# Routing one batch row ahead of the other in a mixture-of-experts stage, with part of its search moved into the attention before it

## The chip, the cores and the metric

One core of one Trainium2 chip runs the whole program in one launch. The metric is the device time of the execution in microseconds (us), the median of three runs. Engines: PE (TensorE), VectorE (DVE in the rows), ScalarE (ACT), GpSimd (POOL) and SyncE (SP); 16 DMA engines move data.

## What is computed

Two batch rows of 1,024 tokens with 128 features pass four residual layers: attention a, a mixture-of-experts feed-forward, attention b, the same feed-forward again. Both attentions have 16 heads of 8 features and are causal.

```python
x = x + attn_a(layernorm(x));  x = x + ffn(layernorm(x))
x = x + attn_b(layernorm(x));  x = x + ffn(layernorm(x))

def ffn(x):                                     # 8 experts, hidden 512
    scores = softmax(einsum('bsd,ed->bse', x, router_w))
    gate, sel = top_k(swapaxes(scores, 1, 2), 257)      # 257 tokens per expert and row
    tokens = x[b, sel]
    h = gelu(tokens @ w1 + b1)
    y = (h @ w2 + b2) * gate[..., None]
    return zeros_like(x).at[b, sel].add(y)
```

An expert takes 257 of the 1,024 tokens of each row. The choice is a top-k over tokens, so nothing can be gathered before all scores of a row are known.

## The kernel before

The kernel writes out the order of each engine by hand. It runs per layer k (0 for a, 1 for b) `project_and_attend` and then `feed_forward`, each a block with its own PSUM banks.

**Attention.** A layer has 16 halves (`HALVES`): a group of four heads of one batch row by the upper or lower 512 queries. A half is 12 or 28 units, 320 in a layer; the second row starts at unit 160, and offsets below are counted from there. A unit is one score product (L1055), one exp on ScalarE (L1141), and every four units the values product (L1073) for a set of keys. Ahead of the scores PE computes all scores once more to find row maxima: pieces (L993), reduced on VectorE (L1164), over a ring of two slots of two PSUM banks (`RINGS`, `mx`). `beside_table` places the pieces; the last of them stands at offset 122. Output turns and the projection of the first row use the ring too. In layer a `PROJECT` puts the first row's projection at offsets 132 and 138, with join, measurement and normalise (L1207, L418 to L451) behind; in layer b the first row's joins, measurements, scale and normalise stand at offset 148.

**Feed-forward: the front.** The normalised input is turned by PE (`turn`, L1443), copied and split in two parts for the fp32r products, and multiplied with the router weights (`logits`, L1450). `keep_busy` (L499) puts idle matmuls in the gaps. Then softmax.

**Search and lists.** Both rows are searched together: 15 steps (`SHIFTS`), each eight small PE products that count (L1466), two VectorE instructions that take the count (L1784, L1786) and two that set up the next one (L1774, L1776). `rank` settles ties, `place` numbers the slots, `make_hot` (L1824, 2,048 elements) lays out one expert's one-hot lanes and `find` (L1507) reads its row numbers. GpSimd gathers by them: first the 257th tokens of all experts (`odd_x`, L1413), then each expert's four index columns (L1400).

**Items.** Three experts are computed densely on all 2,048 tokens, twelve items of 512 (`("dense", q)`, turned back and weighted by a gate that is zero for tokens not chosen, L1847). Five are routed: `("some", s)` holds 258 slots of both rows, in two halves. The order is ten dense, five routed, two dense. An item is four hidden blocks (L1587 dense, L1594 routed) and, after the next item's hidden blocks, four output blocks (L1610, L1615). A block is three products, high by high, high by low, low by high; the units of the stage count blocks, eight per item. ScalarE applies gelu (L1659) and makes the high part (L1666), VectorE the low part (`low`, L1735), which the output waits for. `rows_low`, `scale_back` serve the routed items.

**Two spare banks** carry everything else that PE computes beside the items (`SPARE_AT`): a wait on `spare_done` ahead of each entry. `SPARE_AT` and `vector_events` fix at which unit each entry stands, on PE, ScalarE and VectorE alike; all three work strictly in that order.

**Weights** are in three buffers each; experts 3 to 7 wait until a predecessor has been used.

**The end.** GpSimd adds scaled rows to a DRAM sum (L1408, four per expert, each waiting for the expert before it), then the odd rows (L1422). SP and ScalarE reload the sum (L1391), VectorE adds it to x (L1895), and in layer b SP stores the output.

## Time and profile before

| | us |
|---|---|
| median of 3 runs (978.05 to 980.05) | 979.27 |
| the profiled execution | 978.48 |
| its span | 976.6 |
| PE busy | 840.6 (86%) |
| VectorE busy | 653.0 (67%) |
| ScalarE busy | 565.9 (58%) |
| GpSimd busy | 350.9 (36%) |

A program reads each engine's busy time from one profiled execution. Matmuls overlap in the records, so the mean of one is longer than the distance from one to the next: the distance is what a stretch of products costs, and it is read from the chain, where pieces follow each other without overlap. An idle engine costs nothing by itself; it costs where every other engine waits as well. The stages, by the first and last instruction of each: feed-forward of layer a 336.4 to 506.7, of layer b 810.3 to 976.6.

### The profile page before, as it was taken

To read this page: it belongs to the slowest core of one execution; us is meant where nothing else is said; L and a number is where in the kernel's file an instruction comes from. 1 tells how busy PE (TensorE), PEld (TensorE's weight loads), DVE (VectorE), ACT (ScalarE), POOL (GpSimd) and SP (SyncE) were. 2 spreads that over 40 slices of the span, in tenths; PEclk is the share of its full clock that TensorE was granted. 3 is DMA by queue.
4 is the path that set the end of the run, shared out by engine and by line. 5 is a ranking of instruction groups with operands and counts; after the bars stand their busy time and mean duration, and the time that the engine had idled before them with its cause. 6 is when DMAs were issued, how large, how long until landed. Compare 5 with 4: busy or idle time off the path is not lost. (4 is left out here: it accounts for less than half of the span.)

```text
span 976.6 us, 15787 instructions
## 1 busy us (share of the span) xinstructions
PE 840.6 (86%) x5786; PEld 535.1 (55%) x5786; DVE 653.0 (67%) x1204; ACT 565.9 (58%) x1020; POOL 350.9 (36%) x579
## 2 busy tenths in 40 slices
PE   3888999999999889979937898999999988997992
PEld 1554566556655567769824333444444436676981
DVE  4686667767774457947745877777777745785772
ACT  2524666656666567746705256666666676775661
POOL 1262336656233300186826112133212330008683
PEclk9999999999999989989969799999999999997996
DMA  3662431331111151024424271110000006112444
GB/s 102 185 204 55 143 85 66 98 98 34 66 66 45 59 160 44 22 70 132 54 53 125 69 186 43 34 34 13 22 2 2 1 2 185 55 44 57 138 56 100
DMA packets 57595, 73.57 MB, mean 75 GB/s; under 512 B 11296, under 2 KB 44784, under 8 KB 57136
## 3 DMA queue, kind: packets, MB, share of 16 engines
q1 hardware_dynamic: 43024, 61.42, 21.5%
q0 software_dynamic: 7168, 5.45, 4.2%
q10 hardware_dynamic: 7328, 5.71, 2.1%
q8 instruction: 46, 0.75, 0.3%
q14 instruction: 29, 0.24, 0.1%
HBM read 41.68 MB, written 29.77 MB: 73 GB/s over the span
## 5 line engine op out<-in xcount | busy, mean ns | idle before, releaser
L1141 ACT ACTIVATE b_pt<-b_banks 128x512 f32<-128x512 f32 (+1 forms) x320 | 154.6, 559 | 100.1 <-PE b_banks L1055 99.9
L1164 DVE TENSOR_REDUCE a_mlate<-a_banks 128x2 f32<-128x1024 f32 (+3 forms) x120 | 125.0, 1080 | 50.8 <-PE a_banks L993 32.1
L1164 DVE TENSOR_REDUCE b_mlate<-b_banks 128x2 f32<-128x1024 f32 (+3 forms) x120 | 126.0, 1081 | 35.0 <-PE b_banks L993 18.3
L1055 PE MATMUL a_banks<-a_q,a_k 121*128 121x512 f32 (+3 forms) x384 | 117.4, 383 | 5.5 <-DMA a_q<-a_mt 4.6
L1141 ACT ACTIVATE a_q_hl<-a_banks 128x512 f32<-128x512 f32 (+1 forms) x160 | 81.8, 557 | 68.5 <-PE a_banks L1055 67.0
L1141 ACT ACTIVATE a_k_hl<-a_banks 128x512 f32<-128x512 f32 (+1 forms) x160 | 82.2, 557 | 52.8 <-PE a_banks L1055 51.3
L993 PE MATMUL a_banks<-a_k,a_q 120*128 120x512 f32 (+3 forms) x384 | 99.5, 362 | 11.0 <-DVE a_mlate L1164 7.3
L1055 PE MATMUL b_banks<-b_q,b_k 64*128 64x512 f32 (+3 forms) x384 | 98.1, 413 | 11.7 <-ACT b_pt L1141 8.9
L1659 ACT ACTIVATE f_h<-f_banks,b_t 128x512 f32<-128x512 f32 (+1 forms) x136 | 89.4, 685 | 30.3 <-PE f_banks L1594 17.0
L1055 PEld LDWEIGHTS b_banks<-b_q,b_k 64*128 64x128 f32 x384 | 47.1, 185 | 86.7 <-ACT b_pt L1141 55.3
L1055 PEld LDWEIGHTS a_banks<-a_q,a_k 121*128 121x128 f32 x384 | 65.3, 191 | 50.9 <-issue 20.1
L1610 PE MATMUL f_banks<-f_hr,f_w2r 128*128 128x512 f32 x288 | 81.5, 416 | 6.4 <-DVE f_hr L1735 6.4
L1735 DVE TENSOR_TENSOR f_hr<-f_h,f_hr 128x1024 fp32r<-128x1024 f32 (+1 forms) x68 | 82.8, 1220 | 3.6 <-ACT f_hr L1666 3.5
L919 POOL TENSOR_SCALAR_AFFINE_SELECT b_pt<-b_pt 128x128 f32<-128x128 f32 x128 | 36.9, 293 | 133.9 <-ACT b_pt L1141 133.8
L993 PE MATMUL b_banks<-b_k,b_q 63*128 63x512 f32 (+3 forms) x384 | 75.1, 381 | 9.8 <-DVE b_mlate L1164 6.1
L1587 PE MATMUL f_banks<-f_xr,f_w1r 128*128 128x512 f32 x288 | 80.3, 418 | 0.6 <-ACT f_h L1659 0.6
L1073 PE MATMUL b_banks<-b_pt,vg 128*32 128x512 f32 (+3 forms) x768 | 79.9, 506 | 0.0
L993 PEld LDWEIGHTS a_banks<-a_k,a_q 120*128 120x128 f32 x384 | 64.6, 192 | 26.0 <-DVE a_mlate L1164 15.7
L1408 POOL DMA_INDIRECT scratch_sum<-f_xg,f_index x40 | 69.4, 1735 | 20.6 <-issue 10.4
L1666 ACT ACTIVATE f_hr<-f_h 128x1024 fp32r<-128x1024 f32 (+1 forms) x68 | 72.2, 1062 | 2.2
L1164 DVE TENSOR_REDUCE b_mearly<-b_banks 128x2 f32<-128x768 f32 (+3 forms) x56 | 49.7, 918 | 24.5 <-PE b_banks L1003 23.8
L1164 DVE TENSOR_REDUCE a_mearly<-a_banks 128x2 f32<-128x768 f32 (+3 forms) x56 | 49.7, 916 | 21.9 <-PE a_banks L1003 21.1
(252 smaller groups left out, 1371.0 us busy)
## 6 DMA issues: line engine op xcount, KB each, us to landing
scratch_w<-a_tab SPq DMA_DIRECT2D x16, 512.0 KB, 3.0
f_w1r<-scratch_w SPq DMA_DIRECT2D x16, 512.0 KB, 4.5
f_w2r<-scratch_w SPq DMA_DIRECT2D x16, 512.0 KB, 3.6
a_rot<-in_w SPq DMA_DIRECT2D x16, 256.0 KB, 3.9
a_q<-scratch_q SPq DMA_DIRECT2D x8, 384.0 KB
a_k<-scratch_k SPq DMA_DIRECT2D x8, 384.0 KB
scratch_q<-b_q_hl SPq DMA_DIRECT2D x24, 128.0 KB, 2.8
b_q<-scratch_q SPq DMA_DIRECT2D x32, 96.0 KB
```

Of the source, the lines that this page charges most:

```text
L919: pool.affine_select(out=block[:, 0:P], in_=block[:, 0:P], compare_op=ALU.is_ge, fill=0.0, base=0, pattern=[[1, P]], channel_multiplier=-1 ...
L993: last = pe.matmul(to[:, bank, col:col + w], head_rows(q2, n, h, slice(q * P, (q + 1) * P), 0), head_rows(k2, n, h, slice(k0, k0 + w), 0), ...
L1055: last = pe.matmul(st[u % NST][:, col:col + w], head_rows(k2, n, h, slice(key * P, (key + 1) * P), 1), head_rows(q2, n, h, slice(c * CH + ...
L1073: last = pe.matmul(o_ps[VW * h:VW * (h + 1), q0:CH], vg[n % 2][:, key, h, :], pt[(SET0[i] + s) % NPT][:, h, col:col + w], start=(key == 0) ...
L1141: act.activation(pt[at % NPT][:, h, 0:cols], st[u % NST][:, 0:cols], ACT.Exp, scale=scale).then_inc(exp_done, 1)
L1164: last = dve.tensor_reduce(dst, src, AX.X, ALU.max, negate=True)
L1408: pool.indirect_dma_start(out=sums, out_offset=row(s, c), in_=xg[s][:, c, 0:D], in_offset=None, compute_op=ALU.add).then_inc(scattered[c / ...
L1587: last = pe.matmul(h_ps[:, j, :], w[:, wp, j * P:(j + 1) * P], xr[xp][:, chunk(c)], start=(p == 0), stop=(p == 2))
L1610: last = pe.matmul(y_ps[:, n % 2, :], w[:, wp, j * P:(j + 1) * P], hr[n % 2][hp][:, j, 0:CH], start=(j == 0 and p == 0), stop=(j == HB - 1 ...
L1659: act.activation(to, source, ACT.Gelu, bias=m.b1_t[:, e * HB + j:e * HB + j + 1]).then_inc(gelu_done, 1)
L1666: act.activation(hr[n % 2][0][:, j - 1:j + 1, 0:width], h[n % 2][:, j - 1:j + 1, 0:width], ACT.Copy).then_inc(h_high, 1)
L1735: dve.tensor_tensor(hr[q % 2][1][:, first:end, 0:width], h[q % 2][:, first:end, 0:width], hr[q % 2][0][:, first:end, 0:width].bitcast(F32) ...
```

## The change

Batch row 0 is routed apart from row 1, and ahead of it.

- In the attention's last third (`ROUTE_AT`, `ROUTE_VECTOR`, `ROUTE_SCALAR`, offsets of the second row) the first row goes through projection (layer a, offsets 108 and 111), joins and measurements (110 to 114), scale (115), normalise on ScalarE (117 to 120), turning (123), logits (127), exp (129), softmax and first step (130), and 11 of 15 search steps (133 to 158). The entries use the ring. Its rows and scores are stored to DRAM there, and the sums zeroed.
- Both rows have two dense experts and six routed ones: 8 dense items and 12 routed of 258 columns instead of 12 and 5 of twice 258. Steps are done per row, on half the columns, so 30 in place of 15 in a layer.
- Order: four dense of row 0, six routed of row 0, three dense of row 1, six routed of row 1, one dense.
- The front is gone. The second row's attention output, norm, turning and logits are entries beside the first items (units -1 to 20), its 15 steps start at unit 22, its list is laid out at unit 76 (the first row's at unit 18).
- Lists are made from two digits of 16 (`lists`, `find`, `expand`) for all experts of a row at once; `make_hot` is gone.
- All eight experts' weights have buffers of their own and load in one go. There are two DRAM sums per row, so a scatter waits for the expert before the last, and two DMAs per expert in place of four. The first row's sum is reloaded and added before the last output.
- `keep_busy` is gone from the feed-forward.

The core of the diff:

```diff
-KEEP = 3
-DENSE = KEEP * NCH
-ROUTED = NE - KEEP
...
-AHEAD = 10
-
-ITEMS = [("dense", q) for q in range(AHEAD)] + [("some", s) for s in range(ROUTED)]
-ITEMS += [("dense", q) for q in range(AHEAD, DENSE)]
+DIGITS = 16
+QUAD = 4
+LATE = range(NCH // B, NCH)
+KEEPS = (2, 2)
+
+ITEMS = [("dense", 0, 0), ("dense", 0, 1), ("dense", 1, 0), ("dense", 1, 1)] + [("some", 0, e) for e in range(KEEPS[0], NE)]
+ITEMS += [("dense", 0, 2), ("dense", 0, 3), ("dense", 1, 2)] + [("some", 1, e) for e in range(KEEPS[1], NE)] + [("dense", 1, 3)]
 ITEM = {item: n for n, item in enumerate(ITEMS)}
+SOME = [item for item in ITEMS if item[0] == "some"]
+SOME_AT = {item: i for i, item in enumerate(SOME)}
+KEPT = [item for item in ITEMS if item[0] == "dense"]
+KEPT_ROOM = 4
+TAKE_AT = {(4, 1): 2, (4, 3): 3}
...
+SOME_COST, DENSE_COST, STEP_COST, STEP_EVERY = 0.65, 0.95, 0.4, 2.1
+EARLY_STEPS = 11
+STEPS = len(SHIFTS)
+
...
+def spare_table(k):
+
+    at = [(-1, ("attn", 2)), (-1, ("attn", 3)), (0, ("through", 2)), (1, ("through", 3))] if k == 0 else []
+    for n, item in enumerate(ITEMS):
+        if item[0] == "some":
+            late = 0 if ITEMS[n - 1][0] == "some" else 2
+            at += [(unit_of(n - 1) + 3 + late, ("rows", *item[1:])), (unit_of(n + 2) + 1, ("back", *item[1:]))]
+    first = [(2 * i - 1, ("count", 0, EARLY_STEPS + i)) for i in range(STEPS - EARLY_STEPS)]
+    u = first[-1][0]
+    at += first + [(u + 2, ("rank", 0)), (u + 4, ("place", 0)), (u + 5, ("odd_index", 0)), (u + 11, ("find", 0)),
+                   (u + 13, ("expand", 0))]
+    at += [(13, ("xn", 2)), (14, ("xn", 3)), (18, ("logits", 1))]
+    steps = paced(22, [STEP_EVERY] * (STEPS + 1) + [1.0, 4.5, 1.2])
+    at += [(u, ("count", 1, i)) for i, u in enumerate(steps[:STEPS])]
+    at += list(zip(steps[STEPS:], [("rank", 1), ("place", 1), ("odd_index", 1), ("find", 1), ("expand", 1)]))
+    last = {b: max(ITEM["some", b, e] for e in range(KEEPS[b], NE)) for b in range(B)}
+    after = unit_of(last[0] + 2)
+    at += [(unit_of(6) + 3, ("twins", 0)), (after + 5, ("odd_turn", 0)), (after + 7, ("odd_sum", 0))]
+    for i, item in enumerate(KEPT):
+        b = item[2] // (NCH // B)
+        n = 5 + i if b == 0 else last[0] + 3 + i
+        at.append((max(unit_of(n) + 5, unit_of(ITEM[item] + 2) + 3), ("turn", i)))
+    after = unit_of(last[1] + 2)
+    at += [(unit_of(last[1] - 3) + 5, ("twins", 1)), (after + 3, ("odd_turn", 1)), (after + 4, ("odd_sum", 1))]
+    return sorted(at, key=lambda entry: entry[0])
...
+def vector_events(k):
 
     events = []
     for n in range(len(ITEMS)):
-        for at, first in zip(low_units(n), (0, 2)):
-            events.append((at, 1, "low", (n, first, first + 2)))
-    for i in range(len(SHIFTS)):
-        events.append((FIRST_COUNT + i * COUNT_EVERY, 0, "step", i))
-    events.append((RANK, 0, "rank", 0))
-    events.append((PLACE, 0, "place", 0))
-    for u, keys in BESIDE_UNIT.items():
-        events += [(u, 2 + i / 10, key[0], key[1:]) for i, key in enumerate(keys)]
-    events += [(u, 3, "hot", s) for s, u in HOT_AT.items()]
-    events += [(100, 3, "odd_spread", ()), (112, 3, "odd_gates", ())]
+        for at, first in zip((4, 6), (0, 2)):
+            events.append((unit_of(n) + at, 1, "low", (n, first, first + 2)))
+    events += [(-1, 4, "split", (0,)), (1, 4, "split", (1,)), (unit_of(4) + 5, 4, "split", (2,)), (unit_of(4) + 7, 4, "split", (3,))]
+    if k:
+        events.append((0, 1.5, "join", (2,)))
+    events += [(3, 4, "measure", (2,))] + [(5, 4, "measure", (3,))] * (k == 0)
+    events += [(7, 4, "scale", ()), (8, 4, "norm", (2,)), (8, 5, "norm", (3,))]
+    at = {key: u for u, key in SPARE_AT[k]}
+    for b in range(B):
+        events += [(at["place", b], 3, "lists", (b,)), (at["twins", b] - 5, 4, "odd_spread", (b,)),
...
+ROUTE_AT = {"a": [(108, ("attn_turn", 0)), (111, ("attn_out", 0))], "b": []}
+for _kind in "ab":
+    ROUTE_AT[_kind] += [(123, ("xn_turn", 0)), (127, ("logits", 0))]
+    ROUTE_AT[_kind] += [(133 + 5 * i // 2, ("count", i)) for i in range(EARLY_STEPS)]
+ROUTE_VECTOR = {"a": [(113, "measure", 0), (114, "measure", 1), (115, "scale", 0), (130, "weigh", 0)],
+                "b": [(110, "join", 0), (111, "measure", 0), (112, "join", 1), (113, "measure", 1), (115, "scale", 0),
+                      (130, "weigh", 0)]}
+ROUTE_SCALAR = [(117 + i, "norm", i) for i in range(TT // 2)] + [(129, "exp", 0)]
...
+    def lists(self, dve):
+
+        m = self.m
+        dve.tensor_scalar(m.high_digit[:, :, :], m.slot[:, :, :], 4, None, ALU.logical_shift_right)
+        self.link(dve, dve.tensor_scalar(m.low_digit[:, :, :], m.slot[:, :, :], DIGITS - 1, None, ALU.bitwise_and))
+        numbers = m.steps[:, len(SHIFTS) * PLANES:].rearrange("p (o n) -> p o n", o=1).to_broadcast([P, TT * NE, DIGITS])
+        digit = lambda t: t.rearrange("p t (e o) -> p (t e) o", o=1).to_broadcast([P, TT * NE, DIGITS])
+        self.link(dve, dve.tensor_tensor(self.pairs[:, :, 1, :], numbers, digit(m.high_digit[:, :, :]), ALU.is_equal))
+        dve.tensor_tensor(self.ends, numbers, digit(m.low_digit[:, :, :]), ALU.is_equal)
+        self.link(dve, dve.tensor_scalar(self.pairs[:, :, 0, :], self.pairs[:, :, 1, :], m.token[:, 0:1], None, ALU.mult))
+        ones = self.pairs.rearrange("p (t e) v a -> p t e v a", e=NE)[:, :, :, 1, :]
+        rows = m.tile_row[:, :].rearrange("p (t o q) -> p t o q", o=1, q=1)
+        dve.tensor_tensor(ones, ones, rows.to_broadcast([P, TT, NE, DIGITS]), ALU.mult).then_inc(m.hot_ready, 1)
...
+        early.store_rows(sp, norm)
+        early.store_scores(sp)
+        for b in range(B):
+            for to in m.sums["ab".index(kind)][b]:
+                sp.dma_start(to[0:T, :].rearrange("(t p) d -> p t d", p=P),
...
+        def norm_tiles(first, end):
+
+            act.wait_ge(norm.scaled, NCH // B)
+            for t in range(first, end):
+                act.activation(m.xn[:, t, :], m.x[:, t, :], ACT.Identity, scale=m.sc[:, 2, t:t + 1], bias=m.sc[:, 3, t:t + 1]
+                               ).then_inc(norm.xn_by_act, 1)
...
+        early.wait_lists(pool)
+        early.gather_odd(pool)
+        for e in experts[0]:
+            gather(0, e)
+        pool.wait_ge(m.filled, 16 * 4 * (k + 1))
+        for e in experts[0][:-2]:
+            scatter(0, e)
+        late.wait_lists(pool)
+        late.gather_odd(pool)
+        gather(1, experts[1][0])
+        gather(1, experts[1][1])
+        scatter(0, NE - 2)
+        gather(1, experts[1][2])
+        scatter(0, NE - 1)
+        for e in experts[1][3:]:
+            gather(1, e)
+        scatter_odd(0)
+        for e in experts[1]:
+            scatter(1, e)
+        scatter_odd(1)
...
+        beside(-1)
+        for u in range(LAST_UNIT):
+            n, j = divmod(u + HB, 2 * HB) if u >= HB else (0, u)
+            if j < HB and n < len(ITEMS):
+                hidden(n, j)
+            elif j >= HB:
+                output(n - 1, j - HB)
+            beside(u)
+        for u in range(LAST_UNIT, LAST_UNIT + 2 * HB):
+            beside(u)
...
+        def finish(b):
+            for c in range(b * NCH // B, (b + 1) * NCH // B):
+                dve.wait_ge(m.x_in[c], 32 * (k + 1))
+                early.link(dve, dve.tensor_tensor(flat(m.x, c), flat(m.x, c), landing(c, 0).rearrange("p t n -> p (t n)"), ALU.add))
+                dve.tensor_tensor(flat(m.x, c), flat(m.x, c), landing(c, 1).rearrange("p t n -> p (t n)"), ALU.add
+                                  ).then_inc(finished, 1)
```

`Routing` holds a row's chain (projection to lists) for both places it is called from; each of its counts, `rank` and `place` is an entry of the ring in the attention and of the spare banks in the feed-forward.

## Rows read from the trace of the kernel before

**Rows 1.** The page, busy time: engine, us (share of the span) x instructions.
```profile
PE 840.6 (86%) x5786; PEld 535.1 (55%) x5786; DVE 653.0 (67%) x1204; ACT 565.9 (58%) x1020; POOL 350.9 (36%) x579
```

**Rows 2.** Busy time by stretch: from:to, length, each engine, granted clock, DMA.
```profile
745.00:780.00 35.00, 31.89 (x242) 14.49 (x240) 25.39 (x33) 21.92 (x47) 8.67 (x27) 1.00 0.01 2
336.40:506.70 170.30, 142.09 (x975) 115.94 (x975) 108.90 (x247) 101.58 (x140) 65.11 (x42) 0.91 0.34 85
810.30:824.00 13.70, 13.18 (x104) 11.45 (x104) 9.69 (x38) 8.04 (x16) 0.00 (x0) 1.00 0.79 232
824.00:887.10 63.10, 58.96 (x410) 44.14 (x410) 49.75 (x102) 50.51 (x68) 8.40 (x3) 0.97 0.23 70
887.10:892.40 5.30, 0.00 (x0) 0.00 (x0) 0.25 (x1) 0.52 (x1) 4.08 (x5) 0.63 0.16 40
892.40:957.80 65.40, 64.40 (x447) 56.13 (x447) 43.23 (x89) 41.44 (x56) 50.34 (x34) 0.95 0.40 84
957.80:976.60 18.80, 0.63 (x4) 0.42 (x4) 3.71 (x8) 0.00 (x0) 3.77 (x3) 0.56 0.49 121
```

**Rows 3.** The chain of waits at the first gather, layer b: start, us, what.
```profile
877.31 0.78 issue
878.09 4.49 POOL f_odd_x L1413
882.88 3.17 POOL f_xg L1400
886.35 1.83 POOL f_xg L1400
889.75 2.59 DMA f_xg<-scratch_x,f_index
```

**Rows 4.** The chain at the end of the program.
```profile
966.28 5.44 DMA v<-scratch_sum
```

**Rows 5.** The chain: a search step, three dense products, twelve routed, four transposes.
```profile
855.26 0.22 DVE f_planes L1784
...
856.62 1.14 DVE f_hr L1735
...
861.87 0.70 PE f_banks L1587 x3
...
910.00 0.44 PE f_banks L1554 x4
...
915.25 1.45 PE f_banks L1594 x12
```

**Rows 6.** Busy time by stretch: joins, measurements, scale of layer b's first row.
```profile
786.30:793.60 7.30, 6.00 (x39) 1.93 (x31) 6.63 (x33) 5.04 (x11) 1.23 (x5) 1.00 0.00 0
```

**Rows 7.** The exps (L1141) alone, by stretch of attention b: ACT busy (x count).
```profile
745.00:780.00 35.00, 21.19 (x45) 1.00 0.01 2
780.00:805.00 25.00, 17.41 (x37) 0.96 0.01 2
```

**Rows 8.** Groups by line and shape: count | busy us, mean ns | idle before.
```profile
L1164 DVE TENSOR_REDUCE b_mlate<-b_banks 128x2 f32<-128x1024 f32 x80 | 96.9, 1223 | 21.9 <-PE b_banks L993 18.3 <-PE b_banks L1003 3.7
L1824 DVE TENSOR_TENSOR f_hot<-steps,f_lane 128x2048 bf16<-128x2048 int32 x10 | 22.8, 2280 | 0.1
L1847 DVE SCALAR_TENSOR_TENSOR x<-f_banks,f_gate,x 128x128 f32<-128x128 f32 x96 | 27.0, 344 | 16.4 <-PE f_banks L1554 16.0
L1141 ACT ACTIVATE b_pt<-b_banks 128x256 f32<-128x256 f32 x64 | 20.7, 389 | 18.9 <-PE b_banks L1055 18.8
L444 ACT ACTIVATE xn<-x,sc 128x128 f32<-128x128 f32 x32 | 13.1, 482 | 7.4 <-DVE sc L436 7.4
```

**Rows 9.** DMA issues: what, queue, count, size, median us from issue to landing.
```profile
f_w1r<-scratch_w SPq DMA_DIRECT2D x16, 512.0 KB, 4.5
```

**Rows 10.** Timeline, layer a, first hidden products at the lower clock.
```profile
352.32 6.11 PE L1587 MATMUL f_banks<-f_xr,f_w1r 128*128 128x512 f32 x18
```

**Rows 11.** Timeline, layer a, ScalarE between the exp and the first gelus.
```profile
353.49 1.28 ACT L1659 ACT_TABLE_LOAD   x1
354.78 1.26 ACT L1659 ACTIVATE f_h<-f_banks,b_t 128x512 f32<-128x512 f32 x2
```

More of the change, by code:

```diff
@@ new lines, in vector_events @@
+    events += [(at["logits", 1] + 2, 0, "weigh", ()), (LAST_UNIT - 8, 4, "finish", (0,))]
+    for i, (u, key) in enumerate(SPARE_AT[k]):
+        events.append((u, 2 + i / 1000, key[0], key[1:]))
+    return sorted(events, key=lambda event: event[0:2])
+EVENTS = [vector_events(k) for k in range(2)]
+LOWS = [[arg for _, _, what, arg in EVENTS[k] if what == "low"] for k in range(2)]
+LOW_DONE = [{(n, first): i + 1 for i, (n, first, end) in enumerate(LOWS[k])} for k in range(2)]
+ROUTE_AT = {"a": [(108, ("attn_turn", 0)), (111, ("attn_out", 0))], "b": []}
@@ L1708, in scalar @@
+        for c in range(NCH // B):
+            take_chunk(c)
+        beside(-1)
+        for u in range(LAST_UNIT):
+            n, j = divmod(u + HB, 2 * HB) if u >= HB else (0, u)
+            if j < HB and n < len(ITEMS):
                 bend(n, j)
```

1319 lines of the change are left out of this document (645 added, 674 removed).

## Prediction

> **What bounds the kernel now.** I read the page's busy rows first: PE is busy 86% of the span, more than any other engine [rows 1]. An average doesn't say where it binds, so I then read busy time by stage. In the attention of layer b PE has 31.9 of 35 us and VectorE 25.4, so VectorE has 27% to spare [rows 2]. The feed-forward stage of layer b runs from 810.3 to 976.6, 166.3 us, in five parts: a front of 13.7 (turning the input, logits, softmax, idle matmuls), 63.1 of dense items with the search beside them (PE 59.0), a hole of 5.3 in which PE does nothing, 65.4 with PE busy 64.4, and a tail of 18.8 with PE at 0.6 [rows 2]. Layer a's stage takes 170.3 [rows 2]. The hole is the gather: the chain shows three indirect DMAs of 4.49, 3.17 and 1.83 us issued one behind the other on POOL, and a further one whose transfer takes 2.59 before PE goes on [rows 3]. The tail is scatter, reload (5.44 [rows 4]), add and store. So PE bounds the two long parts, a routing chain the hole, DMA latency the tail.
>
> **PE work removed.** Three 512-column products take 0.70 us, a dense item has 24: 5.6 us. Twelve 258-column products take 1.45, so 0.121 each [rows 5]. Before: 12 x 5.6 + 5 items x 48 x 0.121 = 96.2 us a layer. After: 8 x 5.6 + 12 x 24 x 0.121 = 79.6. That is 16.6 less a layer, and the front, 13.7, goes too. If all of it reached the end, both layers would give 60 us. I don't forecast that, because of what the change puts in their place.
>
> **Attention's last third: +8 us each, +16 in all.** Units of the second row are counted from its start; the last max piece is at unit 122, so VectorE's free stretch begins there. The counts (units 133 to 158) lie in it. But two joins, two measurements and the scale now stand at units 110 to 115, among pieces. In the kernel before this block of layer b took 7.3 us with normalise around it, VectorE busy 6.6 [rows 6], and stood where no piece was; I take 6.3 without the normalise. A unit takes 35/45 = 0.78 us while pieces run and 25/37 = 0.68 when they have ended [rows 7]. Five units are 3.9 us, and three or four pieces at 1.22 [rows 8] are there as well: VectorE has some 11 us of work to unit 115, starts it 2 us in, behind a piece, and ends the scale 13 us after unit 108. ScalarE, which stands at unit 117 with a wait for the scale, would have been there at 8.2. That is a stall of 4.8. Exps and, three units later, score products queue behind this wait. Then ScalarE normalises 8 tiles in four units at 0.48 each [rows 8] less overlap, some 3.3 us against its slack of 0.2 a unit: +2.7. Eleven counts of eight small products, 0.21 to 0.33 each, bring units from 0.68 part of the way to 0.78: +1.9; the pipeline catches up 0.7. Sum +8.7 for b. Layer a has two 1,024-wide steps more on VectorE, but gives back the projection that stood at units 132 to 142: I take +7.3. Bounds for one attention: +2 (the lead of two ring slots hides the block) to +13.
>
> **The stage's opening, to the first routed item: 48 us.** Counted from the stage's start. The first hidden block waits for its weights: 4.5 to landing [rows 9], with issue and release 5.3. PE has stood idle and runs at the lower clock, where 18 products took 6.11, so 1.02 for three, against 0.70 [rows 5, 10]; two blocks, 7.3. From then VectorE has this in order before the list is laid out (unit 18): a joint search step runs from 855.26 to 856.62, where the low behind it starts: 1.36 [rows 5]. With half the columns it lies between 0.68 and 1.36; its four short instructions have a fixed part that doesn't halve, and I take 0.95. Three steps and the short last one 2.65; rank and place 1.35; one split 0.6; the second row's measurement, scale and 8 normalises 5.8; six lows at 1.14, 6.9; the digit lists 4.6; copying the turned input 1.3; odd index, find, expand 1.5. That is 24.7, and with 1.5 for handshakes the list stands at 33.5. In the lists two comparisons have 1,024 elements, half of 2.28 each [rows 8]; the two bf16 multiplies behind them no row shows: between 0.3 and 1.14 each, I take 0.9, nearer to the comparison that they resemble.
> Next the gather: from 877.3, when the index was written, the third indirect DMA started at 886.35, and lands 2.6 later [rows 3]: 11.6, call it 12. So rows at 45.5, while PE has come to unit 25 at some 38: a hole of 7 instead of 5.3. With transposes, copy and split the first routed item starts at 48. Before it started 87 us into the stage, but with ten dense items done; now four are.
> Late in this opening ScalarE makes the second row's exp among gelus. The trace has a table load of 1.28 us with a gelu 0.01 behind it [rows 11]; two loads are 2.6, in the shadow of the gather. The Trainium skill (ScalarE: Activation LUTs, What ACT_TABLE_LOAD costs) adds a drain of about 1.4 us to each switch, so 5.3; that too fits in a hole of 7, and no drain is visible here.
>
> **Six routed items of the first row: 41.5 us.** PE has 6 x 2.9, the dense output before them 2.8, and transposes at 0.11 [rows 5], counts, finds: 32.4. VectorE has more: 12 lows at 0.63 (7.6), 12 search steps at 0.95 (11.4), rank to expand with the lists (7.5), four turns at 1.13 (4.5; four instructions of 0.344 less overlap [rows 8]), row splits and scalings (3.8), input splits (1.3), odd slots (1.6): 37.7. So VectorE becomes the bound. With a tenth lost in handshakes, 41.5. Bounds: 34 (PE's sum) to 49.
>
> **The rest.** Three dense items, PE-bound, 18. Six routed items of the second row: PE 4.0 each, ScalarE four gelus of 258 columns, a copy of 516, twice, keep and rows, from 0.39 for 256 columns [rows 8]: 3.9, and a loop through rows copy and split of 4.7: 28, and 1 for the dense output among them. One dense hidden, 2.8. That is 48 + 41.5 + 18 + 29 + 2.8 = 139.3. Then: last low 3.1, the first row's four adds ahead of the last scaling 2.9, scaling 0.5, two scatters 3.4, the odd scatter 3 with its landing, reload 5.9, adds 2.9, store 2.6: 24.4. The dense chunk's output lies under it. Layer b's stage: 163.7 against 166.3, so **-2.6**. Layer a: VectorE has 3 more ahead of the list (attention output of the second row), and the store is missing: 142.3 + 22.3 = 164.6 against 170.3, so **-5.7**. The weights now load in one stretch without waits and share the DMA engines with the first gathers: 0 to +3, I take 0 because gathers of the kernel before ran beside them too.
>
> **Sum.** Profiled execution 978.5 (span 976.6 and 1.9 around it), 0.8 under the median of 979.3. 978.5 + 16 - 8.3 = **986**.
>
> **Rivals.**
> (1) PE keeps its rate in the stage: lists and steps fit between lows. For it: 16.6 us of removed products a layer, and before the change VectorE stayed at 77% beside the same search. Against: the sum of 37.7. Opening 45, then 34, 17.5, 27, 2.8 and tail 23: 149 for b, 151 for a (-17, -19). With the attention as forecast: 978.5 + 16 - 36 = 958.
> (2) The attention hides its new block (+2 each), stage as forecast: 974.
> (3) Both: 978.5 + 4 - 36 = 946.
> (4) Slower, by the clock. After the gather's hole PE resumes at the lower level, as after the hole before, where the clock of 887 to 892 was 0.63 [rows 2]. Below it PE had 98% to do and the clock came back; now it has 32.4 of 41.5. If it doesn't come back through the six items, PE's 32.4 become 32.4 x 1.02/0.70 = 47, with handshakes 49.5: 8 more a layer, 1002. It decides from where PE at the lower clock is slower than VectorE's 37.7.
>
> **How the numbers follow.** Forecast (977 to 995) 0.44; rival (1) 0.17, (2) 0.15, (3) 0.10, (4) and beyond 0.14. About 0.2% is what a measurement of this kernel can tell from no change, 977.3 to 981.2: it takes 0.06 of the forecast and 0.02 of (2). Faster: 0.17 + 0.10 + 0.13 = 0.40; same 0.08; slower 0.52. The range, 951 to 1004, cuts off most of (3) and what is beyond (4). The forecast's own range is 977 to 995.
>
> **What would show it.** In the changed trace: a ScalarE idle of 4 to 5 us before the first normalise at unit 117; first hidden product about 5 us into the stage; list laid out at 33; PE idle near 7 before the first routed item at 48; VectorE busy over 85% through the first row's six items; a tail of 22 to 24 after the last hidden block. I am wrong if the first routed item starts before 42, if VectorE is under 80% there, or if attention b ends as early as before.

## The result, and the profile after

The changed kernel takes 996.3 us (median of 4 runs, 985.6 to 997.8), the kernel before on the same chip 978.7: a ratio of 1.0167 (95% interval 1.0100 to 1.0235), 1.7% slower. The profiled execution took 995.86, its span 993.9. The forecast was 986, the range 951 to 1004. Line numbers are those of the kernel whose trace is shown.

The page's busy times and granted clock by slice. PE is busy as long as before, 842.8 against 840.6 [rows 1]; the span is 17.3 longer.

```profile
PE 842.8 (85%) x5842; PEld 526.3 (53%) x5842; DVE 667.9 (67%) x1416; ACT 553.1 (56%) x1078; POOL 363.6 (37%) x599
...
PEclk9998999999998898999978799999999856899997
```

The span in parts, the feed-forward stages counted from their first to their last instruction as in [rows 2]:

| us | before | after | change | forecast |
|---|---|---|---|---|
| to the start of stage a | 336.4 | 353.3 | +16.9 (of it 1.1 ahead of the second row) | +7.3 |
| feed-forward a | 170.3 | 158.0 | -12.3 | -5.7 |
| to the start of stage b | 303.6 | 324.7 | +21.1 (of it 20.4 in the second row) | +8.7 |
| feed-forward b | 166.3 | 157.9 | -8.4 | -2.6 |

So the attentions cost 38 instead of 16, the stages give back 21 instead of 8. The misses are 22 and 12, in opposite directions.

**The stages.** Busy time by stretch, as in [rows 2]: from:to, length, then PE, PE's weight loads, VectorE, ScalarE and GpSimd with their instructions, granted clock, DMA share and GB/s. Layer b first: wait for the weights, opening, six routed items of the first row, three dense, six routed of the second row, the last hidden block, tail; then two stretches of layer a (opening, six routed items).

```profile
836.00:839.90 3.90, 0.35 (x9) 0.31 (x9) 2.24 (x8) 2.43 (x3) 0.00 (x0) 0.89 0.74 225
839.90:879.30 39.40, 31.90 (x212) 23.93 (x213) 29.04 (x87) 23.01 (x30) 6.84 (x6) 0.84 0.60 213
879.30:922.20 42.90, 34.57 (x334) 29.42 (x333) 34.30 (x120) 23.20 (x50) 17.08 (x13) 0.96 0.17 23
922.20:941.10 18.90, 18.20 (x95) 13.82 (x91) 10.26 (x18) 15.32 (x23) 15.67 (x11) 1.00 0.25 34
941.10:967.70 26.60, 25.69 (x187) 23.60 (x188) 15.33 (x45) 21.49 (x47) 20.32 (x16) 1.00 0.42 77
967.70:970.80 3.10, 3.10 (x18) 2.53 (x17) 1.67 (x6) 2.68 (x4) 2.49 (x3) 1.00 0.25 21
970.80:993.90 23.10, 8.19 (x34) 5.37 (x32) 9.86 (x18) 3.50 (x6) 9.63 (x6) 0.68 0.51 108
...
353.30:399.00 45.70, 34.29 (x245) 26.58 (x246) 34.49 (x107) 25.73 (x33) 6.75 (x6) 0.89 0.56 203
399.00:442.00 43.00, 33.22 (x336) 27.94 (x334) 34.41 (x120) 23.17 (x50) 17.06 (x13) 1.00 0.16 24
```

The reader is to see that in the six routed items (third row) neither engine is full, PE and VectorE are at 80% each, while in the dense and later routed ones PE is at 96%.

**The opening of stage b.** Timeline of PE, VectorE and GpSimd (start, us, what, idle before and who ended it). PE waits for its weights, then 4.92 for the flags of the 257th tokens (L672), which on VectorE stand behind the second row's scale and its eight normalises (L455). The index is written at 870.0, and the first four gathers that follow take 0.95 to 0.99 each, not the 4.49 and 3.17 of [rows 3]. The lines at 842.88 and 845.86 are the same six products at a granted clock of 0.50 and 0.99.

```profile
839.90 2.90 PE L1794 MATMUL f_banks<-f_xr,f_w1r 128*128 128x512 f32 x6 [3.36 <-DMA f_w1r<-scratch_w]
...
842.88 2.91 PE L1794 MATMUL f_banks<-f_xr,f_w1r 128*128 128x512 f32 x6
...
845.86 1.62 PE L1794 MATMUL f_banks<-f_xr,f_w1r 128*128 128x512 f32 x6
...
855.97 2.13 DVE L455 TENSOR_SCALAR xn<-x,mv,sc 128x128 f32<-128x128 f32 x8
...
858.50 0.20 DVE L672 TENSOR_SCALAR odd_hot<-slot 128x64 bf16<-128x64 int32 x1
...
858.84 0.34 PE L573 MATMUL f_banks<-odd_rows,odd_hot 128*8 128x2 bf16 x8 [4.92 <-DVE odd_hot L672]
...
869.56 0.42 DVE L702 TENSOR_REDUCE index<-v 128x16 int32<-128x256 f32 x1
...
870.92 0.95 POOL L729 DMA_INDIRECT odd_x<-scratch_x,odd_read  x1 [40.69 <-DVE index L702]
872.18 0.99 POOL L723 DMA_INDIRECT f_xg<-scratch_x,index  x1 [0.31 <-issue]
```

**The attention's last third, layer b.** The time of a unit is that of its exp, counted from the exp at offset 0 in the same kernel. At offset 108 both kernels are at 84.5; at 120 before is at 94.5, after at 99.6; at 159, 120.0 against 140.4. Busy time by stretch from offset 108 to 120, to 130, to 140, to 159, of after:

```profile
773.60:788.60 15.00, 12.75 (x82) 5.94 (x79) 12.93 (x43) 8.08 (x19) 3.94 (x12) 0.77 0.01 2
788.60:799.30 10.70, 9.43 (x59) 5.40 (x58) 3.06 (x6) 6.48 (x15) 0.00 (x0) 0.78 0.17 50
799.30:812.00 12.70, 12.30 (x68) 4.46 (x69) 4.42 (x19) 5.33 (x13) 1.17 (x4) 0.50 0.63 169
812.00:829.50 17.50, 16.71 (x129) 8.33 (x129) 6.97 (x28) 9.04 (x21) 6.56 (x18) 0.50 0.00 0
```

and the same four stretches of the kernel before:

```profile
768.10:778.20 10.10, 9.08 (x81) 4.60 (x77) 7.17 (x11) 5.87 (x14) 3.93 (x12) 1.00 0.01 2
778.20:785.40 7.20, 5.50 (x41) 2.17 (x37) 1.50 (x2) 5.58 (x12) 0.00 (x0) 1.00 0.01 1
785.40:792.90 7.50, 6.44 (x41) 2.41 (x42) 6.17 (x30) 5.24 (x12) 1.17 (x4) 1.00 0.01 2
792.90:803.60 10.70, 8.61 (x65) 3.66 (x65) 3.41 (x12) 8.68 (x20) 6.10 (x18) 0.98 0.00 0
```

Three things add up. In the first stretch VectorE is at 86% and PE stops. In all the others PE, not ScalarE, is the busiest engine (before, the two had 20.6 and 19.5 of the 25.4 us behind offset 120). And in the last two the granted clock is 0.50, its 1.2 GHz level: the low stretch begins at 794.7 and lasts 37.5 us without a break, with PE busy at 95 to 97% from 799.3 on.

The stop itself, from the timelines of VectorE, PE and ScalarE: measurement and scale stand between pieces (L1444), PE waits 2.03 at a piece, ScalarE 2.16 for the scale. The clock falls at 781.0 for 6.8 us, 0.8 behind the end of PE's stop.

```profile
777.27 0.87 DVE L422 BATCH_NORM_STATS2 st<-x 128x6 f32<-128x128 f32 x4
778.06 0.36 DVE L425 BATCH_NORM_AGGREGATE mv<-st 128x2 f32<-128x6 f32 x4
778.45 0.40 DVE L427 TENSOR_SCALAR sc<-mv 128x4 f32<-128x4 f32 x1
778.88 1.23 DVE L1444 TENSOR_REDUCE b_mearly<-b_banks 128x2 f32<-128x1024 f32 x1
780.02 0.68 DVE L462 TENSOR_TENSOR x<-x,xn 128x512 f32<-128x512 f32 x1
...
780.16 0.50 PE L1257 MATMUL b_banks<-b_k,b_q 63*128 63x384 f32 x4 [2.03 <-DVE b_mearly L1444]
...
785.80 0.88 ACT L1393 ACTIVATE xn<-x,sc 128x128 f32<-128x128 f32 x2 [2.16 <-DVE sc L440]
```

### The profile page after: what moved, and what is told of

Read it like the earlier page. It is cut to its first block and busy times, and to the rows that moved or that the text cites. A ratio compares the mean times of both kernels' runs of the same rounds, so it can differ in the third digit from the quotient of the medians.

```text
span 993.9 us, 16405 instructions
## 1 busy us (share of the span) xinstructions
PE 842.8 (85%) x5842; PEld 526.3 (53%) x5842; DVE 667.9 (67%) x1416; ACT 553.1 (56%) x1078; POOL 363.6 (37%) x599
## 5 line engine op out<-in xcount | busy, mean ns | idle before, releaser
L1444 DVE TENSOR_REDUCE a_mlate<-a_banks 128x2 f32<-128x1024 f32 (+3 forms) x120 | 124.9, 1080 | 52.7 <-PE a_banks L1257 33.3
L1444 DVE TENSOR_REDUCE b_mlate<-b_banks 128x2 f32<-128x1024 f32 (+3 forms) x120 | 125.8, 1080 | 33.9 <-PE b_banks L1257 17.4
L1326 PE MATMUL b_banks<-b_q,b_k 64*128 64x512 f32 (+3 forms) x384 | 104.4, 442 | 10.3 <-ACT b_pt L1417 7.2
L1669 POOL DMA_INDIRECT scratch_sum<-f_xg,index x48 | 82.2, 1713 | 63.5 <-DVE f_xg L1931 31.1
L1806 PE MATMUL f_banks<-f_hr,f_w2r 128*128 128x258 f32 (+1 forms) x480 | 105.2, 355 | 0.0
L1834 ACT ACTIVATE f_h<-f_banks,b_t 128x258 f32<-128x258 f32 (+1 forms) x160 | 82.8, 555 | 34.3 <-PE f_banks L1794 33.8
L1326 PEld LDWEIGHTS b_banks<-b_q,b_k 64*128 64x128 f32 x384 | 50.8, 201 | 91.1 <-ACT b_pt L1417 49.3
L1344 PE MATMUL b_banks<-b_pt,vg 128*32 128x512 f32 (+3 forms) x768 | 87.2, 546 | 0.0
L1894 DVE TENSOR_TENSOR f_hr<-f_h,f_hr 128x516 fp32r<-128x516 f32 (+1 forms) x80 | 71.8, 904 | 20.4 <-ACT f_hr L1841 19.9
L1257 PEld LDWEIGHTS a_banks<-a_k,a_q 120*128 120x128 f32 x384 | 65.4, 195 | 30.2 <-DVE a_mlate L1444 16.2
L1806 PEld LDWEIGHTS f_banks<-f_hr,f_w2r 128*128 128x128 f32 x480 | 75.4, 199 | 8.5 <-issue 1.0
L1841 ACT ACTIVATE f_hr<-f_h 128x516 fp32r<-128x516 f32 (+1 forms) x80 | 64.4, 805 | 2.5
L1444 DVE TENSOR_REDUCE b_mearly<-b_banks 128x2 f32<-128x768 f32 (+3 forms) x56 | 49.7, 917 | 23.1 <-PE b_banks L1267 22.4
L1444 DVE TENSOR_REDUCE a_mearly<-a_banks 128x2 f32<-128x768 f32 (+3 forms) x56 | 49.7, 917 | 19.9 <-PE a_banks L1267 19.2
```

The lines of the kernel that those rows point to most:

```text
L1257: last = pe.matmul(to[:, bank, col:col + w], head_rows(q2, n, h, slice(q * P, (q + 1) * P), 0), head_rows(k2, n, h, slice(k0, k0 + w), 0), ...
L1326: last = pe.matmul(st[u % NST][:, col:col + w], head_rows(k2, n, h, slice(key * P, (key + 1) * P), 1), head_rows(q2, n, h, slice(c * CH + ...
L1344: last = pe.matmul(o_ps[VW * h:VW * (h + 1), q0:CH], vg[n % 2][:, key, h, :], pt[(SET0[i] + s) % NPT][:, h, col:col + w], start=(key == 0) ...
L1444: last = dve.tensor_reduce(dst, src, AX.X, ALU.max, negate=True)
L1669: pool.indirect_dma_start(out=sums[b][i], out_offset=routes[b].row(e, c), in_=xg[b, e][:, c, 0:D], in_offset=None, compute_op=ALU.add).the ...
L1806: last = pe.matmul(y_ps[:, n % 2, 0:width(n)], w[:, wp, j * P:(j + 1) * P], hr[n % 2][hp][:, j, 0:width(n)], start=(j == 0 and p == 0), st ...
```

## The experiments

All were timed beside the kernel before, whose median was 976.4 to 977.2. Each has one trace, of one of its runs. The theory behind them: the attention's loss is a stop (VectorE's block among the pieces), added PE work where PE is the bound, and a stretch at the lower clock; the stage is set by VectorE up to the last of the first row's routed items.

**The changed kernel once more** (no edit).

> The changed kernel itself, once more, beside the two others. Theory 1 (the long stretch at TensorE's lower clock in layer b's last third comes in some executions and not in others, and costs 8 to 10 us where it comes): times in two groups about 10 apart, near 986 and 996, and the spans go with the mean clock. Theory 2 (it is the change's own, in every execution): one group near 996.

987.0, 994.8, 994.9 and 996.5; ratio 1.0169 (1.0127 to 1.0211). With the four runs above: two near 986, six between 994.8 and 997.8. The profiled one (994.8) has a stretch of 37.5 at the lower clock again, in the same place. Seven traces of this study have the changed kernel's block, turning and logits at its offsets: four have the stretch with 37.5 us, one with 17.1, two not at all. Theory 1, as far as it goes: both traces of the changed kernel are of runs in the slower group, so that the faster one lacks the stretch is inferred. The mean granted clock agrees: 0.938 and 0.932 in the two faster runs, 0.917 to 0.927 in the six others. Other kernels vary by some 10 us for other reasons too (of turns_late, below, the traced run has the stretch and is the fastest of four).

**Filling PE's stop.**

```diff
                 pe.wait_ge(exp_done, u - NST + 1)
+            if 112 <= u - UNIT0[2 * NG] < 120:
+                keep_busy(pe, m, st[u % NST][:, 0:2 * P], 3)
```

> The changed kernel with three idle 256-column products ahead of each score product at offsets 112 to 119 (24, about 2.8 us of PE in each attention, placed where PE waits for VectorE). Theory 1 (PE's idle 2.0 us at a piece is what precedes the fall of the clock in layer b's last third): no long stretch at the lower clock there, -8 to -10, 987. Theory 2 (the idle time there has nothing to do with the clock): the same low stretch, and 0 to +4 for the added products, 996 to 1000.

984.4 (980.6 to 992.0), about 11 under the changed kernel. The first row is offset 108 to 120, the second 140 to 159:

```profile
769.00:783.90 14.90, 14.64 (x106) 7.34 (x104) 13.18 (x43) 8.49 (x19) 4.30 (x12) 1.00 0.01 2
...
803.80:817.10 13.30, 11.45 (x131) 6.24 (x130) 7.35 (x29) 8.79 (x21) 6.63 (x18) 1.00 0.02 5
```

The added products cost nothing (99.5 at offset 120 against 99.6 without them): they lie in the stop. The clock stays at 1.00 from offset 108 to 120, and the last stretch takes 13.3 for the work that took 17.5. The fall in between, which every trace with the stop shows some 13.7 us behind the first, is there as well, at 790.5 for 6.8 us. Theory 1 for the first fall. For the long stretch one trace can't tell a cure from luck: two of the seven traces with the stop lack it too, and filled's second row (132.6 at offset 159) is only 0.5 shorter than theirs (133.1). The four times are under six of the eight of the changed kernel, 2 under its two faster ones in the median.

**The stop alone, in the kernel before.**

```diff
+                for _ in range({110: 2, 112: 2, 113: 2, 115: 3}.get(UNIT0[i] + v - UNIT0[2 * NG], 0)):
+                    link(dve.tensor_tensor(extra[:, 1, :], extra[:, 0, :], extra[:, 0, :], ALU.add))
```

> The kernel before with nothing but nine additions of 512 elements on VectorE (0.69 us each, on a tile of their own) at offsets 110 to 115 of the second row in both attentions, among the last row-maximum pieces: a stand-in for the joins, measurements and scale. Theory 1 (VectorE's work among the pieces stops PE, and that stop by itself can send TensorE's clock to its lower level for some 37 us): 4 to 5 us a layer, 985 to 987, and in some executions 8 to 10 more. Theory 2 (the stop costs its own time alone; the long stretch needs the turning and the small logits products that follow it in the changed kernel): 985 to 987 in all executions, no low stretch over 14 us in the trace of layer b's last third.

986.0 (983.7 to 991.7), ratio 1.0096 (1.0062 to 1.0130). PE stops twice at a piece:

```profile
780.06 0.50 PE L994 MATMUL b_banks<-b_k,b_q 63*128 63x384 f32 x4 [1.15 <-DVE b_mearly L1165]
...
783.18 0.80 PE L994 MATMUL b_banks<-b_k,b_q 63*128 63x512 f32 x2 [1.42 <-DVE b_mt L1179]
```

The clock falls at 782.3, between the two stops (in the seven traces above 0.6 to 1.8 us behind the stop of 2.03), but for 6.8 us only, and once more for 3.4. The second rows end 4.9 (a) and 5.8 (b) later. So the stop costs 5 to 6 us a layer by itself, the short falls of the clock included. The seven times spread over 8 us, wider than either theory had it, but not in two groups, and the trace has no long stretch: theory 2. The first fall comes with the stop (the kernel before has none from offset 0 until 119.5 us behind it, at its last unit); the long stretch was seen only where turning and logits follow it.

**No early steps.** The stage's four steps start the search; the first row's choice is then its first 257 tokens instead of the best ones.

```diff
-    ROUTE_AT[_kind] += [(133 + 5 * i // 2, ("count", i)) for i in range(EARLY_STEPS)]
...
-        self.reach_out(dve, 0)
+        self.reach_out(dve, 0 if self.b else EARLY_STEPS)
```

> The changed kernel without the 11 early search steps of the first row (the row's choice then starts from the last four steps and is its first 257 tokens; nothing else is left out). Theory 1 (PE is the bound there, so each step costs its eight products, 0.36 us, and some of the wait for VectorE): 4 to 7 us a layer, 984 to 988, and below 980 if the steps are also what holds the clock of layer b at its lower level. Theory 2, the forecast's (ScalarE is the bound, 11 steps cost 1.9 a layer): 992.

Two groups: five runs at 975.6 to 976.3, five at 984.3 to 987.3 (its trace, of the second group, has the 37.5). The changed kernel has 986 and 996, so the totals differ by some 10.5, 0.48 us for each of 22 steps. The traces, both with the long stretch, put less of it where the steps stood: the second row of layer a ends 5.4 earlier (0.49 a step), that of layer b 2.2 (0.20); the rest lies elsewhere. Theory 1 for the total and for layer a; the forecast had 0.17. And the steps are not what holds the clock down: without them it is at its lower level for 37.5 us all the same.

**The block earlier.**

```diff
-                "b": [(110, "join", 0), (111, "measure", 0), (112, "join", 1), (113, "measure", 1), (115, "scale", 0),
-                      (130, "weigh", 0)]}
-ROUTE_SCALAR = [(117 + i, "norm", i) for i in range(TT // 2)] + [(129, "exp", 0)]
+                "b": [(50, "join", 0), (56, "measure", 0), (62, "join", 1), (68, "measure", 1), (74, "scale", 0),
+                      (104, "weigh", 0)]}
+ROUTE_SCALAR = [(78 + i, "norm", i) for i in range(TT)] + [(101, "exp", 0)]
```

> The changed kernel with the first row's projection, join, measurement, scale, normalise, turning and logits moved from offsets 108-130 to 50-104 of the second row, one tile normalised per unit; the 11 steps stay where they are. Theory 1 (joins, measurements and scale of VectorE between the last row-maximum pieces hold PE at a piece, and ScalarE behind it): the 8.2 us (layer a) and 5.1 us (layer b) lost between offsets 110 and 120 go, about -12, so 984; and if the long stretch at the lower clock in layer b (37 us) is a consequence of that stop, about 10 more go, 974. Theory 2 (the work only moves, since VectorE is as full between offsets 50 and 104): 994 to 998.

981.4 (975.9 to 985.6), ratio 1.0043 (1.0005 to 1.0081): 13 to 15 less than the changed kernel's medians. In layer b the units lose 0.0 up to offset 72, so both joins and measurements are free; 3.5 from there to 84 (scale and normalises); 5.5 from 92 to 104 (turning, logits, exp, softmax), PE at 98% there. In both the clock falls for 6.8 us. The first line is most of offsets 72 to 84, the second 92 to 104; the third is offset 92 to 104 of all_early (below), with the same turning, logits and exp and without a fall:

```profile
741.00:751.00 10.00, 9.04 (x53) 4.16 (x51) 7.34 (x21) 4.67 (x12) 2.79 (x8) 0.67 0.01 2
...
761.30:775.80 14.50, 14.26 (x88) 7.46 (x87) 9.37 (x14) 6.55 (x13) 2.81 (x8) 0.76 0.01 2
```

```profile
753.60:765.20 11.60, 11.36 (x90) 6.36 (x87) 8.49 (x10) 6.52 (x13) 2.78 (x8) 1.00 0.01 2
```

The kernel before takes 9.0 there. So turning, logits and what follows them cost 2.6 where the clock stays up, and the fall 2.9 more.

Between the two theories: in layer b nothing was saved net but the long low stretch (133.5 at offset 159, against 133.1 in the two traces that lack it), since block, turning and logits cost 8.6 where they went, the two falls included; layer a's second row is 5.6 shorter.

**Slots before the second row's normalise.**

```diff
-    events += [(7, 4, "scale", ()), (8, 4, "norm", (2,)), (8, 5, "norm", (3,))]
+    events += [(11, 4, "scale", ()), (11, 4.1, "norm", (2,)), (11, 4.2, "norm", (3,))]
```

> The changed kernel with the second row's scale and eight normalises on VectorE moved from units 7 and 8 to unit 11, behind the first row's slots and lists. Theory 1 (the 4.9 us in which PE stands in the opening of each feed-forward stage are VectorE's fourteen short scale and eight normalise instructions ahead of the odd slots): the stop shrinks to under 1, the index is written 4 us earlier, -3 to -4.5 a layer, so 988. Theory 2 (PE then stands for the second row's turning, or for the gathered rows, because VectorE's sum to the index is the same): within 1.5 of the changed kernel, 995 to 997.

996.6 (993.2 to 1009.6), no gain. Counted from PE's first instruction of stage b, as for every index time in this section, the index comes at 34.2 instead of 33.8, and PE stops elsewhere, for the turning and for the gathered rows:

```profile
855.59 1.15 PE L1729 MATMUL f_banks<-ident,xn 128*128 128x128 f32 x4 [5.80 <-DVE xn L455]
...
872.39 0.43 PE L1766 MATMUL f_banks<-ident,f_xg 128*128 128x128 f32 x2 [2.38 <-issue]
```

Theory 2: the opening is VectorE's sum, and an order moves the hole, not the end; the stages came out 4.3 (a) and 4.8 us (b) longer, the total no longer. This trace has no long low stretch, though, and so prices it. Its last three stretches of layer b's second row (offset 120 on):

```profile
790.60:801.10 10.50, 9.26 (x61) 5.14 (x61) 3.19 (x6) 6.51 (x16) 0.00 (x0) 0.83 0.18 51
801.10:810.90 9.80, 9.00 (x70) 3.55 (x71) 4.51 (x19) 5.16 (x12) 1.17 (x4) 0.83 0.81 216
810.90:824.10 13.20, 11.35 (x129) 6.12 (x127) 7.36 (x29) 8.77 (x21) 6.63 (x18) 1.00 0.01 3
```

33.5 against 40.9 in the changed kernel's trace: the long low stretch is 7.4. Against the kernel before, 25.4, it is 8.1 more, and PE's busy time there is 29.6 against 20.6, 9.1 more (the windows' sums). Not all of that is added work: turning (1.05), logits (1.95) and 88 products of counts (3.93) are 6.9, and the rest is old products in the 6.8 us at the lower clock from 797.6 on. An estimate from other traces comes out alike: 2.6 for turning and logits and 2.9 for a fall of 6.8 us (early_block beside all_early), 11 steps at 0.25 (all_early): 8.2. So about two thirds of the 8.1 are PE's added products and one third is the clock.

**Each step's flags twice.**

```diff
+        if self.b:
+            self.link(dve, reach())
+        reach().then_inc(m.count_ready, 1)
```

> The changed kernel with the second row's flags of each step written twice by VectorE (one more instruction of 0.36 us in each of 15 steps, 12 of them beside the six routed items). Theory 1 (VectorE is the bound of that stretch): it grows by all of it, 12 x 0.4 = 4.8, two layers and the rest about +10, 1006. Theory 2 (the two engines wait for each other, neither is full: VectorE is idle 8.6 of 42.9 there): VectorE's idle time takes most of it, under +4, 997 to 1000.

**Steps further apart.**

```diff
-SOME_COST, DENSE_COST, STEP_COST, STEP_EVERY = 0.65, 0.95, 0.4, 2.1
+SOME_COST, DENSE_COST, STEP_COST, STEP_EVERY = 0.65, 0.95, 0.4, 2.8
```

> The changed kernel with the second row's 15 steps 2.8 instead of 2.1 apart (estimated us in the table), so that its last three steps, ranks and lists lie in the three dense items (units 71 to 89) instead of the last routed ones (units 55 to 76). Theory 1 (through the first row's six routed items VectorE and the wait for it set the pace: 34.3 us of VectorE in 42.9, and PE waits 5.5 for the flags of a step): some 7 us of VectorE leave the stretch, it takes 37 to 39, the dense items, where VectorE is busy 10.3 of 18.9, grow by 1 or 2: -3 to -5 a layer, 987 to 991. Theory 2 (the waits move along with the steps and PE waits in the dense items instead): within 2 of the changed kernel.

**Turned dense outputs later.**

```diff
+        u = 82 + 6 * i if b == 0 and i < KEPT_ROOM else max(unit_of(n) + 5, unit_of(ITEM[item] + 2) + 3)
+        at.append((u, ("turn", i)))
```

> The changed kernel with the four turned dense outputs of the first row (16 VectorE instructions of 0.34 us) moved from units 45 to 69, beside the six routed items, to units 82 to 100, beside the three dense ones. Theory 1 (VectorE sets the pace through the six routed items, and the dense ones have room: 10.3 of 18.9): the stretch of six shrinks by 3.5 to 4.5, the dense one stays, -3.5 a layer, about 7 in all. Theory 2 (as with the steps in spread, what is moved is paid where it goes): six items -4, dense items +3 to +4, total within 2.

These three belong together. Six routed items of the first row in layer b, each kernel's own stretch: of twice; of spread, with the three dense and the six routed items of the second row behind; of turns_late, with the three dense.

```profile
874.90:921.70 46.80, 36.87 (x336) 31.77 (x334) 38.38 (x132) 23.51 (x50) 16.51 (x13) 0.89 0.15 21
```

```profile
873.70:910.60 36.90, 30.98 (x294) 26.59 (x295) 29.12 (x103) 22.58 (x50) 19.90 (x15) 1.00 0.19 27
910.60:935.30 24.70, 21.24 (x142) 16.57 (x139) 16.75 (x38) 15.84 (x22) 8.02 (x8) 0.93 0.11 17
935.30:967.10 31.80, 28.46 (x188) 25.96 (x187) 15.14 (x44) 21.69 (x47) 24.23 (x18) 0.89 0.38 69
```

```profile
871.00:910.90 39.90, 30.36 (x320) 26.14 (x318) 30.18 (x104) 23.05 (x50) 17.08 (x13) 1.00 0.17 25
910.90:930.60 19.70, 19.22 (x106) 15.25 (x103) 13.43 (x30) 15.09 (x21) 16.53 (x11) 1.00 0.23 32
```

| | VectorE busy | the six items |
|---|---|---|
| twice | 38.4 (+4.1) | 46.8 (+3.9) |
| changed kernel | 34.3 | 42.9 |
| turns_late | 30.2 (-4.1) | 39.9 (-3.0) |
| spread | 29.1 (-5.2) | 36.9 (-6.0) |

The stretch follows VectorE's work nearly one to one although VectorE is only 80% busy. Two cautions. Turns_late and spread take work from PE as well: in layer a, with a clock of 1.00 in all three, PE's busy time falls from 33.2 to 30.4 and 31.0, so turns_late (42.9 to 39.9) can't tell the two engines apart; spread's 6.0 are more than PE lost. Twice adds to VectorE alone, but at a lower clock, 0.89; the unedited stretch took 43.7 at 0.92 against 42.9 at 1.00, so up to 1 us of its 3.9 may be the clock's. With what is left, some three quarters of the added VectorE time reach the stretch. That is theory 1 for the stretch. The totals differ: spread takes 1002.8 (995.0 to 1005.6), since the dense items grew by 5.8 and the list, now 6 us later, made the second row's gathers late (5.2 more). Turns_late takes 988.6 (986.2 to 1000.4) against 994.8 beside it (987.0 to 996.5): 6 less, near theory 1's 7, though the runs overlap; its dense items grew by 0.8. Twice has a median of 995.5, no more than the changed kernel and less than either theory had, though each of its stages is longer, by 4.2 in layer a and 3.5 in layer b; its trace had 17.1 of the long low stretch instead of 37.5, which hid it. For a difference this small the stretch is the measure, not the total.

**All 15 steps and an easier block in the attention.**

```diff
-EARLY_STEPS = 11
+EARLY_STEPS = 15
...
+    ROUTE_AT[_kind] += [(93, ("xn_turn", 0)), (98, ("logits", 0))]
+    ROUTE_AT[_kind] += [(116 + 3 * i, ("count", i)) for i in range(EARLY_STEPS)]
...
+                "b": [(37, "join", 0), (43, "measure", 0), (49, "join", 1), (55, "measure", 1), (62, "scale", 0),
+                      (105, "weigh", 0)]}
+ROUTE_SCALAR = [(66 + 3 * i, "norm", i) for i in range(TT)] + [(102, "exp", 0)]
```

> As early_block, with the joins and measurements at offsets 37 to 55, the scale at 62 where no piece follows for three units, one normalise every three units from 66 on, and all 15 steps of the first row in the attention, from offset 116, three units apart. Theory 1 (the moved block costs by where it meets pieces and the exps' slack; a step costs its eight products; the stage's opening is VectorE's sum up to the index): block 3 us less than in early_block in each attention, four more steps +1.5, index written 4 to 5 us earlier in each stage: 981 - 2 x 6 = 969. Theory 2 (the opening is bound by PE or the weights, and the attention by the turning and logits whatever the rest does): 978 to 984.

975.6 (967.5 to 981.0), ratio 0.9990 (0.9956 to 1.0025): as fast as the kernel before. Offset 108 to the end of layer b, then the opening of stage b up to the first routed item:

```profile
767.50:806.80 39.30, 34.42 (x342) 17.01 (x339) 22.82 (x74) 25.45 (x54) 11.83 (x34) 1.00 0.25 69
813.90:851.60 37.70, 30.25 (x188) 23.42 (x189) 27.51 (x77) 25.36 (x33) 10.14 (x9) 0.82 0.68 250
```

Against 35.5 of before, fifteen steps cost 3.8, 0.25 each, with no fall of the clock in that stretch. The index comes 24.2 us into stage b instead of 33.8, but the first routed item only 5.4 earlier, after 37.7. PE stands 3.9 us for the second chunk's split (L1906, behind the lists on VectorE) until 826.75; from there to the routed item it waits 0.6 in all, so its dense items are the limit there. Between the two theories (969; 978 to 984).

**The same with the second row's steps further apart** (`STEP_EVERY` 2.6).

> all_early with the second row's steps 2.6 instead of 2.1 apart. If both parts bring what theory 1 says of spread and all_early, 961 to 964; if only one does, 969 to 980.

981.5 (977.0 to 990.0), above both forecasts: spreading the steps costs 6 here, and cost 6 to 8 above.

**The best version**: all_early with the edit of turns_late, and

```diff
-    events += [(-1, 4, "split", (0,)), (1, 4, "split", (1,)),
+    events += [(-1, 4, "split", (0,)), (-1, 5, "split", (1,)),
```

> all_early (975.6) with the turned dense outputs moved as in turns_late, and the split of the second chunk of the first row ahead of its lists on VectorE, since PE stood 3.9 us in each stage for the first hidden product of the second item behind it. Theory 1: -3.5 and -3.5 a layer, 962. Theory 2 (the opening's VectorE sum is unchanged, so PE only stands later, and the turns cost as much where they go): 972 to 976.

972.1 (965.1 to 979.3, 12 runs) against 976.4; ratio 0.9950 (0.9923 to 0.9976). It beats the kernel before by 0.5%. The six items shrink to 41.6 in layer b (clock 0.92) and 39.9 in layer a (0.96), the opening not at all (38.8): in layer b the PE stop of 3.9 before the second dense item became one of 2.2 before an output and one of 0.8 for the lists, again for VectorE. The total is theory 2's, the six items are between the two.

## Why the prediction came out as it did

The sign and the range held, and the mechanism put first (VectorE's block stalls the attention, VectorE sets the stage's first half) is there. The 986 was 10 low by two errors of 22 and 12 that partly cancelled; that the range held is in part that luck.

**Attention, the stop.** Forecast: ScalarE idle 4.8 before the first normalise at unit 117. Found: 2.16, and before it PE's own stop at a piece, which had cost ScalarE 3.65 already. Right in place and cause, and near in size: with the normalises the forecast had 7.5 by offset 120, measured are 5.1 in layer b and 8.2 in layer a, and stop_only gives 5 to 6 for the stop alone.

**Attention, everything behind it: the step that failed.** The forecast priced the rest as ScalarE's (normalises 2.7, counts 1.9) because it took ScalarE for the engine without slack, and gave the first row's turning and logits, 8 and 16 products, no price at all. With [rows 2] at 31.9 of 35 for PE, and with PE and ScalarE nearly even behind the last piece (20.6 and 19.5 of 25.4), the sum had to be made on PE. Made there, layer b without the long low stretch has 9.1 us more PE busy time behind offset 120, 6.9 of it added products, and takes 8.1 longer. Steps were put at 0.17 each; no_steps gives 0.20 (layer b) to 0.49 (layer a) in place, all_early 0.25 where they are spread further.

**The clock.** Rival (4) had a slower outcome by the clock, 8 a layer, in the wrong place, and that its size resembles the 7.4 found is chance. It rests on 1.02 for three products at the lower level, but of the 6.11 us of [rows 10] only the first 3.7 are at that level (the clock was low from 349.2 to 356.0); the trace after has 2.91 against 1.62 for six, a ratio of 1.8 where the forecast used 1.5. In the six routed items the clock is back at 0.96 and 1.00. It stayed down in layer b's attention, after PE's stop, for 37.5 us and 7.4 of time. In place of the forecast's +8.7 layer b has 5.1 (the stop) + 8.1 (products and a short fall) + 7.4 = 20.6; by the units at offset 159 it is 20.4. How long the clock stays down was no term of the sum, and what decides it stays open.

**The opening: 48 forecast, 43.3 found in layer b, 45.7 in a.** The list, forecast at 33.5, was written at 34.0: the sum over VectorE held. First hidden product 3.9 in, not 5.3. Wrong was the gather, 12 with [rows 3] and then 2.5: it took 9.3 in all, because none of its indirect DMAs repeated the 4.49 and 3.17. The hole was not at the gather but at the 257th tokens, 4.9. Two table loads of 1.28 stand around the second row's exp; a gelu starts 0.01 behind the second. The Trainium skill (ScalarE: Activation LUTs, What ACT_TABLE_LOAD costs) adds a drain of about 1.4 us to each load; behind the second there is no room for it, and behind the first ScalarE waits 2.21 for VectorE anyway. No idle of PE in the opening is put down to them.

**Six routed items: 41.5 forecast, 42.9 and 43.0 found.** The size is right. The sign I had set, VectorE over 85%, was not met: it is at 80.0%, on the line under which the forecast was to count as wrong. Busy share was the wrong test. PE waits 5.5 us for VectorE's flags there; VectorE's own idle time of 8.6 is mostly for ScalarE's part of the gathered rows (6.0, f_xs L1864) and hardly for PE (0.5). An engine can set the pace with such holes. Adding to it alone is the right test, and twice says VectorE, for three quarters of what was added.

**The rest.** Three dense 18.9 against 18; the second row's six 26.6 against 29 (PE is at 96% there, so the loop of 4.7 through rows, copy and split did not set the pace); hidden 3.1 against 2.8; tail 23.1 against 24.4. Rival (1), PE keeps its rate, was right in the last half of the stage and wrong in the first.

## What to carry to other kernels

Find the busiest engine of the very stretch into which work is moved, and sum on it every instruction that comes along, the small ones too; a gap in another engine does not help there. Compare stretches at the same granted clock, or price the difference first. An engine at 80% can still set the pace, and adding a known amount to it alone tells more than its busy share; an edit that moves work of two engines at once doesn't tell which of them it was. Order alone moves a hole; removing or relocating the work to a stretch with room shortens it. A short stop of PE can cost more than its length (stops of 1.15 and 1.42 cost 5.8), so work of VectorE that PE waits for belongs where no such wait is queued.
